# Gram tiles' low parts formed on GpSimd from ScalarE's copies, and the image attention's operations dealt out singly behind maxima steps 2 to 9

## What is computed

```
# layer 0
x = x + (attend(q, k[:77], v[:77]) + attend(q, k_ip[77:], v_ip[77:])) @ Wo.T + bo
# layer 1, text rows t = context[:-4], image rows n = context[-4:]
probs_t = softmax(q @ k_t * D**-0.5)
text_out = probs_t @ v_t
qsem = l2norm(probs_t @ t)                         # [S, 512] per head
sem = qsem @ l2norm(n)
probs_ip = softmax(q @ k_ip * D**-0.5 + 0.5 * sem) * spatial_mask
out = (text_out + probs_ip @ v_ip) @ W_out + b_out + x
```

## Time and profile before

| | |
|---|---|
| median of 3 runs | 2523.54 us (2521.98 to 2524.99) |
| the profiled execution, its time | 2525.83 us |
| its span | 2524.0 us |
| PE (TensorE matmul) busy | 2444.6 us, 97% |
| DVE (VectorE) busy | 1642.0 us, 65% |
| ACT (ScalarE) busy | 1228.2 us, 49% |
| POOL (GpSimd) busy | 774.2 us, 31% |
| granted TensorE clock, mean | 0.996 |

### The profile page before, as it was taken

How to read it: one execution, slowest core, us unless ns; L and a number is a source line. 1 busy time by engine, 2 the same in 40 slices (tenths; PEclk the granted TensorE clock), 3 DMA queues, 4 the chain that set the end, 5 groups by cost and what they waited for, 6 DMA issues and landing times.

```text
span 2524.0 us, 64056 instructions
## 1 busy us (share of the span) xinstructions
PE 2444.6 (97%) x26372; PEld 2117.5 (84%) x26372; DVE 1642.0 (65%) x3313; ACT 1228.2 (49%) x2251; POOL 774.2 (31%) x1030
## 2 busy tenths in 40 slices
PE   7899999999999999999999999999999999999998
PEld 6788888888888888888888888888888888888877
DVE  4456667666667666667656677566677666677665
ACT  3355444455444455444554454554454554444543
POOL 3133233233233232233232233332332332332322
PEclk9999999999999999999999999999999999999999
DMA  8865446674556754557655466645566655566620
GB/s 216 139 100 88 93 88 98 106 116 75 88 90 96 117 90 85 89 92 113 104 81 97 80 106 104 108 76 91 97 97 105 98 82 91 88 97 103 95 28 18
DMA packets 371689, 241.44 MB, mean 96 GB/s; under 512 B 131947, under 2 KB 365243, under 8 KB 371388
## 3 DMA queue, kind: packets, MB, share of 16 engines
q1 hardware_dynamic: 371398, 237.35, 56.6%
HBM read 171.35 MB, written 64.59 MB: 93 GB/s over the span
## 4 chain that ended last, share of the span: by engine, by line
PE 71%; DVE 17%; POOL 4%; DMA 2%; SPq 2%; issue 2%; ACT 1%; DVEq 0%; POOLq 0%; ACTq 0%
PE ST L832 7%; PE R L898 5%; PE R L763 5%; PE PN L871 5%; PE R L708 4%; DVE m L1090 4%; POOL w L1468 4%; PE R L776 4%; PE R L777 4%; PE R L709 4%; PE R L956 3%; DVE m L1094 3%; PE PN L916 3%; DVE w L992 3%; PE R L779 3%; PE R L711 3%
## 5 line engine op out<-in xcount | busy, mean ns | idle before, releaser
L1468 POOL TENSOR_TENSOR w<-w 128x448 f32<-128x448 f32 (+1 forms) x256 | 331.2, 1294 | 376.8 <-DVE w L989 358.0
L992 DVE SCALAR_TENSOR_TENSOR w<-p,pr 128x1344 f32<-128x1344 f32 x160 | 295.9, 1850 | 164.6 <-ACT pr L1352 151.0
L1324 ACT ACTIVATE p<-ST 128x1344 f32<-128x1344 f32 x260 | 335.5, 1290 | 99.0 <-PE ST L835 94.0
L989 DVE TENSOR_TENSOR rem<-R,kst 128x298 f32<-128x298 f32 (+2 forms) x180 | 89.4, 497 | 426.5 <-ACT kst L1207 426.3
L898 PE MATMUL R<-pr,Gh 128*128 128x448 f32 (+1 forms) x960 | 366.3, 382 | 0.0
L989 DVE TENSOR_TENSOR w<-R,w 128x448 f32<-128x448 f32 (+1 forms) x480 | 281.7, 620 | 69.4 <-PE R L903 59.2
L1400 POOL TENSOR_TENSOR kst<-rem,kst 128x298 bf16<-128x298 f32 (+2 forms) x180 | 148.0, 822 | 558.1 <-ACT kst L1207 305.2
L776 PE MATMUL R<-wvh,ch 128*128 128x320 f32 (+3 forms) x896 | 302.9, 338 | 0.0
L777 PE MATMUL R<-wvh,cl 128*128 128x320 f32 (+3 forms) x896 | 277.4, 310 | 0.0
L832 PE MATMUL ST<-Qs,Ks 100*128 100x112 bf16 (+1 forms) x3520 | 228.9, 214 | 8.2 <-ACT p L1324 2.7
L832 PEld LDWEIGHTS ST<-Qs,Ks 100*128 100x128 bf16 (+1 forms) x3520 | 187.9, 98 | 46.7 <-issue 13.4
(11 more groups left out here) (230 smaller groups left out, 5768.4 us busy)
## 6 DMA issues: line engine op xcount, KB each, us to landing
Ks<-k_split SPq DMA_DIRECT2D x384, 140.6 KB, 5.8
Ks<-k_split SPq DMA_DIRECT2D x384, 93.8 KB, 8.2
w<-in_ctxT SPq DMA_DIRECT2D x31, 750.0 KB, 10.1
k_split<-kst SPq DMA_DIRECT2D x64, 281.2 KB
k_split<-kst SPq DMA_DIRECT2D x64, 223.5 KB, 3.0
Qs<-q_split SPq DMA_DIRECT2D x64, 210.0 KB, 9.0
q_split<-qst SPq DMA_DIRECT2D x128, 84.0 KB, 2.3
Qs<-q_split SPq DMA_DIRECT2D x64, 140.0 KB, 9.1
```

The source lines that it names most:

```text
L989: return e.tensor_tensor(to, x, y, op)
L992: return e.scalar_tensor_tensor(out=to, in0=x, scalar=s, in1=y, op0=op0, op1=op1)
L1324: e.activation(to.rearrange("p (u q) -> p u q", u=3), st, ACT.Exp).then_inc(p_whole, 1)
L1468: e.tensor_tensor(first, first, w2[n % 2][0:ROWS[j], QW * j:QW * j + QW], ALU.add).then_inc(ns_added, 1)
```

## The change

1. For each Gram tile ScalarE now copies the whole of what is wanted from the bank of R into a slot of rem (the diagonal block halved), and then makes Gh from that copy. The bank is free once the copies are made (`g_read` in place of `g_lo`). GpSimd forms Gl as rem - Gh and copies g4's columns from rem; for t = 2 it also adds the cross products, four operations in all. VectorE's stage `g` is gone. The ring of two rem slots is now shared by keys and Gram tiles.
2. `fuse` and `ip_softmax` are cut into eight stages with one operation of VectorE each (`root_inverse`, `sem`, `fuse`, `fuse_max`, `fuse_less`, `ip_sum`, `ip_inverse`, `ip_softmax`), which `between` takes behind steps 2 to 9. ip_T, ip_mm, o_T and o_mm come behind steps 12, 13, 14 and 16. The value and Gram tiles stand behind steps 2, 3, 5, 6, 8, 11, 12 and 14. The last item keeps its order by a table of its own.

The core of the diff:

```
@@ values
                 o.add("g", b, t)
-                in_bank(("g", b, t), "g_lo", o.at("g", b, t))
+                in_bank(("g", b, t), "g_read", o.at("g", b, t))
+                o.share("rem", 2, ("g", b, t), "g_lo", o.at("g", b, t))
@@ finish1
-        o.add("fuse", b)
-        yield
-        o.add("ip_softmax", b)
-        yield
+        for step in ("root_inverse", "sem", "fuse", "fuse_max", "fuse_less", "ip_sum", "ip_inverse", "ip_softmax"):
+            o.add(step, b)
+            yield
@@ between
-            if count[0] in (1, 2, 3, 5, 7, 9, 10):
+            if b + 1 == B:
+                take(last, (0, 1, 5, 3, 0, 1, 0, 1, 0, 1, 1)[count[0]])
+            elif count[0] in (1, 2, 3, 4, 5, 6, 7, 8, 9, 12, 13, 14, 16):
                 take(last, 1)
-            if count[0] in ((2, 3, 4, 6, 8, 12, 14, 16) if 0 < b < B - 1 else (2, 4, 6, 8, 11, 12, 14, 16)):
+            if count[0] in ((2, 3, 5, 6, 8, 11, 12, 14) if 0 < b < B - 1 else (2, 4, 6, 8, 11, 12, 14, 16)):
                 take(pieces, 1)
@@ vector: the stage "g" (Gl and, for t = 2, g4, from the bank of R) is removed
@@ scalar, stage "g"
-                    copy(Gh[0:n, q:q + n], ps[:, 0:n], 0.5)
-                    if gw > n:
-                        copy(Gh[0:n, q + n:q + gw], ps[:, n:gw])
-                    copy(g4[0:n, t, :], ps[:, gw:gw + NIP]).then_inc(g_hi, 1)
+                    copy(rm[0:n, 0:n], r[0:n, 128 * t:128 * t + n], 0.5)
+                    if t == 2:
+                        copy(rm[0:n, n:n + 1 + 2 * NIP], r[0:n, T - NIP:T + 1 + NIP])
+                        copy(rm[0:n, 128:128 + n + NIP], r[0:n, 0:n + NIP]).then_inc(g_read, 1)
+                    else:
+                        copy(rm[0:n, n:gw + NIP], r[0:n, 128 * t + n:T]).then_inc(g_read, 1)
+                    w.wait_ge(g_read, at("g", b, t))
+                    copy(Gh[0:n, q:q + gw], rm[0:n, 0:gw]).then_inc(g_hi, 1)
@@ gpsimd, new stage "g"
+                    w.wait_ge(g_hi, i)
+                    if b:
+                        w.wait_ge(w4_copied, b)
+                    if t < 2:
+                        e.tensor_copy(g4[0:n, t, :], rm[0:n, gw:gw + NIP])
+                        less(low, rm[0:n, 0:gw], Gh[0:n, q:q + gw].bitcast(fp32)).then_inc(g_lo, 1)
+                    else:
+                        less(low, rm[0:n, 0:gw], Gh[0:n, q:q + gw].bitcast(fp32)).then_inc(g_part, 1)
+                        e.tensor_tensor(g4[0:n, 2, :], rm[0:n, n:n + NIP], rm[0:n, n + 1 + NIP:n + 1 + 2 * NIP],
+                                        ALU.add).then_inc(g_part, 1)
+                        w.wait_ge(g_part, 2 * b + 1)
+                        e.tensor_tensor(low, rm[0:n, 128:128 + n], low.bitcast(fp32), ALU.add)
+                        w.wait_ge(g_part, 2 * b + 2)
+                        e.tensor_tensor(g4[0:n, 2, :], rm[0:n, 128 + n:128 + n + NIP], g4[0:n, 2, :],
+                                        ALU.add).then_inc(g_lo, 1)
```

More of the change, by code:

```diff
@@ L434, in stage_order @@
         take(rows0, 9)
-        for n in (17, 0, 0, 2, 5, 3, 0):
+        for n in (17, 0, 0, 0, 0, 0, 0, 0, 0, 2, 5, 3, 0):
             take(last, 1)
@@ L568, in xattn_two_layers @@
             sem(n) for n in ("c_hi", "c_low", "c_image", "wk_hi", "wk_low", "c_pads"))
-        g_mm, g_hi, g_lo, g4_scaled, w4_copied = (sem(n) for n in ("g_mm", "g_hi", "g_lo", "g4_scaled", "w4_copied"))
+        g_mm, g_read, g_hi, g_part, g_lo, g4_scaled, w4_copied = (
+            sem(n) for n in ("g_mm", "g_read", "g_hi", "g_part", "g_lo", "g4_scaled", "w4_copied"))
         s_max_mm, s_max_read, m_T, m_hi, m_low = (
@@ L578, in xattn_two_layers @@
                              "ip_mm", "ip_added", "num_read"))
+        root_inverted, ip_max, ip_summed, ip_inverted = (
+            sem(n) for n in ("root_inverted", "ip_max", "ip_summed", "ip_inverted"))
         o_T, o_T_copied, o_mm, x_added, x1_T, x1_T_copied = (
@@ L1171, in vector @@
                         ALU.max).then_inc(d_bound, 1)
+                elif kind == "root_inverse":
+                    b, = key
+                    w.wait_ge(d_root, b + 1)
+                    e.reciprocal(sm[0][:], d2[:]).then_inc(root_inverted, 1)
+                elif kind == "sem":
+                    b, = key
+                    f1 = fus[1]
+                    w.wait_ge(root_inverted, b + 1)
+                    tt(f1[:], num[:], sm[0][:].unsqueeze(2).to_broadcast([S, H, NIP]), ALU.mult).then_inc(num_read, 1)
                 elif kind == "fuse":
@@ L1174, in vector @@
                     f0, f1 = fus
[L1175 to L1178, removed]
                     w.wait_ge(num_read, b + 1)
                     tt(f0[:], f1[:], sip[b % 2][:], ALU.add).then_inc(fused, 1)
+                elif kind == "fuse_max":
+                    b, = key
                     w.wait_ge(fused, b + 1)
-                    e.reduce_max(sm[1][:], f0[:], X).then_inc(dve_step, own.one())
-                    w.wait_ge(dve_step, own.n)
-                    tt(f1[:], f0[:], sm[1][:].unsqueeze(2).to_broadcast([S, H, NIP]), ALU.subtract).then_inc(fus_less, 1)
+                    e.reduce_max(sm[1][:], fus[0][:], X).then_inc(ip_max, 1)
+                elif kind == "fuse_less":
+                    b, = key
+                    f0, f1 = fus
+                    w.wait_ge(ip_max, b + 1)
+                    tt(f1[:], f0[:], sm[1][:].unsqueeze(2).to_broadcast([S, H, NIP]), ALU.subtract).then_inc(fus_less, 1)
+                elif kind == "ip_sum":
+                    b, = key
+                    w.wait_ge(ip_exp, b + 1)
+                    e.reduce_sum(sm[1][:], fus[0][:], X).then_inc(ip_summed, 1)
+                elif kind == "ip_inverse":
+                    b, = key
+                    w.wait_ge(ip_summed, b + 1)
+                    e.reciprocal(sm[2][:], sm[1][:]).then_inc(ip_inverted, 1)
                 elif kind == "ip_softmax":
@@ L1187, in vector @@
                     f0, f1 = fus
[L1188 to L1192, removed]
+                    w.wait_ge(ip_inverted, b + 1)
                     if b:
@@ L1272, in scalar @@
                     n, gw, q = ROWS[t], T - 128 * t - NIP, GO[t]
-                    ps = R[slot["R", ("g", b, t)]][0:n, 128 * t:T]
+                    r, rm = R[slot["R", ("g", b, t)]], rem[slot["rem", ("g", b, t)]]
                     w.wait_ge(g_mm, at("g", b, t))
+                    free(w, "rem", ("g", b, t))
                     if b:
                         w.wait_ge(y_mm, 3 * NG * b)
-                        w.wait_ge(w4_copied, b)
-                    copy(Gh[0:n, q:q + n], ps[:, 0:n], 0.5)
-                    if gw > n:
-                        copy(Gh[0:n, q + n:q + gw], ps[:, n:gw])
-                    copy(g4[0:n, t, :], ps[:, gw:gw + NIP]).then_inc(g_hi, 1)
+                    copy(rm[0:n, 0:n], r[0:n, 128 * t:128 * t + n], 0.5)
[6 more added lines that the diff above has]
+                    copy(Gh[0:n, q:q + gw], rm[0:n, 0:gw]).then_inc(g_hi, 1)
                 elif kind == "w4":
@@ L1384, in scalar @@
                     e.preload_act_table(ACT.Exp)
-                elif kind == "fuse":
+                elif kind == "fuse_less":
                     b, = key
@@ L1402, in gpsimd @@
             for kind, key in o.stages:
-                if kind == "w4":
+                if kind == "g":
+                    b, t = key
+                    n, gw, q = ROWS[t], T - 128 * t - NIP, GO[t]
+                    rm, low, i = rem[slot["rem", ("g", b, t)]], Gl[0:ROWS[t], GO[t]:GO[t] + T - 128 * t - NIP], at("g", b, t)
+                    w.wait_ge(g_hi, i)
[13 more added lines that the diff above has]
+                                        ALU.add).then_inc(g_lo, 1)
+                elif kind == "w4":
                     b, = key
```

20 lines of the change are left out of this document (1 added, 19 removed).

## The result

The change made the kernel slower: 2669.62 us median of 4 runs (2660.77 to 2671.45) against 2523.11 us, a ratio of 1.0566 (95% interval 1.0551 to 1.0581). That is 146.5 us more. The direction was forecast, the size was not: 2606 us was forecast, and the range ended at 2634.

A forecast was written before the change was run, and what follows sets the result against it. TensorE was taken to bound the groups, with other engines' effects only in the maxima stage. 29 stages at 2.81 us plus 0.9 gave 82.4 us over the median 2523.54, so 2606 us, range 2574 to 2634.

The forecast's parts named there:

- The bound: Whole item: groups are TensorE's alone; other engines' gains or losses fall in the maxima stage, 24.50 us, TensorE busy 23.42.
- the first part: Stage start to the end of g2's products: s7 at 9.55 us, s11 at 14.48, g2's end at 15.89 instead of 18.13.
- the queue behind g2: v(0,2) waits for v(0,1)'s bank behind ScalarE's and GpSimd's chain; copied 6.84 us after g2, so v(0,2) starts at 22.78.
- The end of the stage: From v(0,2)'s start at 22.78 us through s15, s16 and o_mm, ending at 27.31 against 24.50.
- 4.53: Time in us from v(0,2)'s start to stage end: 2.05, then s15 0.48, s16 0.32 and o_mm 1.68.
- No DMA is moved but the item's output: Load queue: only the output leaves later, some 9 us, and is waited for an item on; no further cost.
- the 82 us forecast: Whole kernel: 29 stages at 2.81 us more, 81.5, and 0.9 for b = 30, giving 82.4 us more.
- 2.81: Extra us per maxima stage in the 29 items that split a context: end at 27.31 against 24.50.
- (a): Maxima stage: only VectorE paces it, GpSimd's chain is hidden; 27 us more, 2551 us; chance 0.10.
- (b): At s11 and v(0,2): VectorE's relief pays, 32 us less, 2491 us; chance 0.05.
- (c): Chain behind g2: GpSimd held twice for 1.12 us each, 2.24 more per stage, 2671 us; chance 0.07.
- The relief of VectorE: Maxima stage: 1.63 us of Gl's operations leave VectorE; worth at most TensorE's idling, 1.08 us times 30, 32 us.

The follow-up runs named there:

- w4_late: The change with g4's scaling and its copy into V1 moved behind the copies of v(0,1) and v(0,2); 2586.41 us, 1.0237 of the kernel before.
- warm: The change with seven unread products put on TensorE between o_T and v(0,2), filling the bank wait; 2634.19 us, 1.0426 of the kernel before.
- out_late: The change with an item's output issued by SP behind the next xT load, not ahead of it; 2631.29 us, 1.0406 of the kernel before.
- gpsimd_only: Only part 1 of the change (GpSimd forms Gl), with the stage order of the kernel before; 2520.42 us, 0.9974 of the kernel before.
- repacked2: The change's part 1 with fillers reordered, g4's scaled copy at the stage's end, m_split right behind m_T; 2521.43 us, 0.9985 of the kernel before.
- repacked2_dve: The order of repacked2, but VectorE forms Gl and g4 as before the change; 2563.21 us, 1.0151 of the kernel before.
- repacked3: repacked2 with o_mm behind step 16 and the output issued behind xT; 2492.29 us, 0.9872 of the kernel before.
- order_only: Only part 2 of the change (its stage order), with VectorE and ScalarE forming Gl and g4 as before; 2654.26 us, 1.0517 of the kernel before.

## Why the prediction was right or wrong

**The bound, the first part, the queue behind g2: right.** s7, s11, g2's end and v(0,2) came within 0.42 us of the sums, GpSimd's four operations took 1.00 us ahead of the split instead of 1.20, the waits 0.88 (1.1 forecast), 0.73 (1.0) and 1.66 (1.9). w4_late and warm show the bank wait's worth, 51 us in the stages, apart from what follows it.

**The end of the stage: wrong, in the term "4.53".** The working took v(0,2), s15, s16 and o_mm at the durations of the earlier trace rows, where TensorE had been busy throughout. The forecast put three waits, 4.0 us in all (3.3 measured), within some 9 us ahead of them, and did not ask for the clock behind them; it is at the lower level in 23 of 29 items. The term measured 5.6 to 7.2 us where it fell, 4.30 with the wait filled. Over all items it is 42 us in the stages, and 35 us of the kernel's time by warm.

**"No DMA is moved but the item's output": wrong.** The text named the output's move and looked for who waits for the output. It should have looked for what stands behind it on SP's queue: xT, which the queries want 3 us after the stage. 38 us, by out_late; 40 in the groups of the profile. With it falls the sentence that another engine's work is gained or lost in the maxima stage alone.

**The account.** By the profile the account closes: to the 82 us forecast come 42 for the clock and 40 for xT, and off go 20, since without the low clock a stage lost 2.1 us and not 2.81. That is 144, the difference of the two spans. So the two terms that were missing, 73 us by the runs, hid that the terms that were there came out too high: without the two the kernel would take some 2596 us and not 2606, which the range holds.

**The rivals.** (a) and (b) did not happen. (c) gave 2671 us, and the time measured is 2670: a coincidence. Its mechanism, GpSimd held twice for 1.12 us, is refuted by the rows of GpSimd above (0.39, 0.20, 0.40, 0.21 and 3.52 for the split): nothing in this chain was held at a port.

**The relief of VectorE** was priced at most 32 us. In the old order it is 5 us (gpsimd_only against the kernel before); in the order of repacked2 it is 42 us (against repacked2_dve). The bound of 32 was TensorE's idling in the old order and holds for that alone. repacked3 as a whole gains 32 us on the kernel before.

**What stays open.** The runs do not tell why some items keep the full clock and others do not, with the same waits. The gains of the single runs (38 + 83) and the rest of 15 leave 10 us of the 146.5: w4_late is worth 93 us in the stages, and its groups give some of this back while xT is still waited for.

## What to carry to other kernels

When a stage is moved in a list that feeds several in-order queues, go down each queue, the load queue too, and ask of every instruction behind the moved one who wants it; the moved one's own reader is seldom the one that suffers. Count a bank's ring as part of the order: two tiles that take turns of three apart are harmless neighbours until two short users slip in between. And price the work behind a new wait of TensorE at both levels of the clock: a wait of 48 us in all brought some 40 us more behind it.

## What the runs showed of the hardware

With waits of 0.88, 0.73 and 1.66 us within 9 us, TensorE's granted clock fell to 0.50 in 23 of 29 items and stayed at 1.00 in the rest, the kernel and place being the same; with only the first two waits (w4_late) it stayed at 1.00 to the end of the stage in 28 of 28. Shorter waits did it too where they stood close together: 0.44, 0.31 and 0.80 us within 3 us in 13 of 29 stages (order_only), 0.45 and 0.30 within 1.4 us in 4 of 29 (repacked2_dve). A single one of 1.7 to 2.1 us did it in three items of w4_late. Products that nobody reads, in an idle wait, made the kernel 35 us faster. GpSimd's additions and subtractions of 115 x 4 and 115 x 115 elements take 0.20 and 0.39 us: by these two rows some 0.2 us is a fixed part, nearly all of the first and half of the second (an estimate), so small operations on GpSimd are priced by their number.
